# Moving the layer-norm centring of an attention stage from ScalarE to VectorE, and a copy to a later place in VectorE's order

## What is computed

```python
mod = (_silu(L0_c) @ L0_wmod).reshape(L0_c.shape[0], 6, 1, -1)
sa, ca, ga, sb, cb, gb = (mod[:, 0], mod[:, 1], ...)
h = _layernorm(x, axis=-1) * (1 + ca) + sa
x = x + ga * _L0_attn_ref(h, L0_attn_w_qkv, L0_attn_w_out)
h = _layernorm(x, axis=-1) * (1 + cb) + sb
x = x + gb * _L0_ffn_ref(h, ...)
```

## Time and profile before

| | |
|---|---|
| median of 3 runs | 1188.49 us (1187.46 to 1189.24) |
| the profiled execution's own time | 1188.49 us |
| span of its instructions | 1186.6 us |
| mean granted TensorE clock | 0.939 of full speed |
| busy share PE, DVE, ACT, POOL over the span | 90%, 79%, 78%, 74% |

### The profile page before, as it was taken

The page is one execution under the profiler, slowest core; times in us unless marked ns, Lnnn a source line. Parts: engine busy times, 40 slices in busy tenths (PEclk is TensorE's granted clock), DMA queues, the critical chain, the costliest instruction groups (busy, mean ns, idle before and its releaser), DMA issues. The chain is left out here.

```text
span 1186.6 us, 51662 instructions
## 1 busy us (share of the span) xinstructions
PE 1067.6 (90%) x18513; PEld 866.7 (73%) x18513; DVE 940.0 (79%) x4130; ACT 923.6 (78%) x3404; POOL 876.9 (74%) x732
## 2 busy tenths in 40 slices
PE   4799999999999999999999999748989985499994
PEld 2577877777777777877877877536867774488883
DVE  6888989889889888988989886547878764288885
ACT  2699999999999999999999997746866652266662
POOL 2788888888878888888888875454677677167777
PEclk9899999999999999999999998969988875699997
DMA  6777777776776777776767776262242122666210
GB/s 194 200 187 169 191 176 170 183 188 165 192 178 168 183 180 171 189 180 165 195 172 173 175 181 161 68 217 72 66 133 95 57 83 108 192 193 185 80 33 31
DMA packets 111036, 181.02 MB, mean 153 GB/s; under 512 B 19726, under 2 KB 64177, under 8 KB 110656
## 3 DMA queue, kind: packets, MB, share of 16 engines
q1 hardware_dynamic: 102944, 158.53, 52.4%
q0 software_dynamic: 6400, 16.82, 3.9%
q10 hardware_dynamic: 1440, 2.36, 0.7%
HBM read 35.20 MB, written 24.73 MB: 51 GB/s over the span
## 5 line engine op out<-in xcount | busy, mean ns | idle before, releaser
L621 POOL TENSOR_TENSOR qk<-mm,sw 128x1024 f32<-128x1024 f32 x128 | 305.9, 2390 | 92.5 <-DMA sw<-mm 92.1
L692 ACT ACTIVATE pr<-sm,mn 128x96 f32<-128x96 f32 x1024 | 368.5, 370 | 0.3 <-DVE mn L522 0.3
L503 DVE TENSOR_TENSOR mm<-bank,cos 128x512 f32<-128x512 f32 x256 | 175.1, 684 | 77.3 <-PE bank L325 64.8
L627 POOL TENSOR_TENSOR pr<-pr,ri 128x768 f32<-128x768 f32 x128 | 188.3, 1471 | 32.0 <-DVE ri L531 31.2
L692 ACT ACTIVATION_READ_ACCUMULATOR pr<-sm,mn 128x1 f32 x1024 | 201.6, 197 | 0.0
L522 DVE CUSTOM_DVE_ANT_0 sm<-bank,msk 128x96 f32<-128x96 f32 x1024 | 191.1, 252 | 1.6 <-PE bank L337 1.6
L504 DVE TENSOR_TENSOR mm<-bank,sin 128x512 f32<-128x512 f32 x256 | 174.1, 680 | 0.0
L702 ACT ACTIVATE pT<-bank 96x512 f32<-96x512 f32 x256 | 137.1, 586 | 15.3 <-PE bank L352 13.4
L368 PE MATMUL bank<-pT,vw 96*64 96x64 f32 x4096 | 148.3, 226 | 0.6 <-issue 0.6
L368 PEld LDWEIGHTS bank<-pT,vw 96*64 96x64 f32 x4096 | 130.6, 138 | 10.6 <-ACT oth L711 1.0
L337 PEld LDWEIGHTS bank<-qk 64*64 64x64 f32 x4096 | 90.8, 133 | 54.3 <-issue 53.1
(11 more groups left out here) (210 smaller groups left out, 2484.6 us busy)
## 6 DMA issues: line engine op xcount, KB each, us to landing
sw<-mm SPq DMA_DIRECT2D x512, 128.0 KB, 2.4
vw<-vn SPq DMA_DIRECT2D x128, 192.0 KB, 2.6
vw<-vn SPq DMA_DIRECT2D x128, 128.0 KB, 2.4
rr<-sorted_scratch SPq DMA_DIRECT2D x72, 192.5 KB, 2.8
vw<-vn SPq DMA_DIRECT2D x96, 64.0 KB, 2.4
xt<-in_x SPq DMA_DIRECT2D x16, 256.0 KB, 3.7
x_scratch<-x SPq DMA_DIRECT2D x16, 256.0 KB, 2.7
rr<-x_scratch SPq DMA_DIRECT2D x16, 256.0 KB, 3.0
```

The source lines that it names most:

```text
L503: dve.tensor_tensor(mm[s % 2][:, 0, j, :], PJ[u % 2][:, :], cos[:, :], ALU.mult)
L621: pool.tensor_tensor(qk[i % 2][:, :, 32:], mm[i % 2][:, 0, :, :], sw[i % 2][:, :, :], ALU.add)\
L627: pool.tensor_tensor(t, t, ri[i % 2][:, :].unsqueeze(2).to_broadcast([P, 8, WK]), ALU.mult)\
L692: ins = act.activation(pr[i % 2][:, h, p, :], ms_[i % 2][:, h, p, :], ACT.Exp, scale=-1.0, bias=mn[i % 2][:, h, p:p + 1], accum_out=sums[i ...
```

## The change

It has three parts in the steady loop, and one of small instructions.

1. `centre` for batches 1 to 15 leaves ACT, where it was four activations of 128x128 with scale `lnr` and bias `lnb`, two at the end of slot r = 0 and two at the end of r = 1. It becomes four DVE instructions of 128x128 (subtract the mean, multiply by `lnr`), all at the end of slot r = 1. Both the input `xt` and the output `hh` are read and written through a view that takes the 64 even channels first and then the 64 odd ones. Batch 0's centring was on DVE already and takes the new view too.
2. POOL no longer computes `lnb`: two small instructions for each batch go, and the counts of `s_ln` follow.
3. On DVE the copy of ACC to `yt` moves from ahead of the maxes to behind the reciprocal, in the same slot r = 6.

```diff
-        lnb = sbt(p1, "lnb", [P, 4])
                 def centre(b):
-                    dve.wait_ge(s_ln, 4 * b + 2)
+                    dve.wait_ge(s_ln, 2 * b + 2)
+                    if b:
+                        dve.wait_ge(s_xn, b)
                     for j in range(4):
-                        ins = dve.tensor_scalar(hh[:, j, :], xt[b % 4][:, j, :], mv[:, j, 0:1], lnr[:, j:j + 1],
-                                                ALU.subtract, ALU.mult)
+                        o, x = (v.rearrange("p (a k) -> p k a", k=2) for v in (hh[:, j, :], xt[b % 4][:, j, :]))
+                        ins = dve.tensor_scalar(o, x, mv[:, j, 0:1], lnr[:, j:j + 1], ALU.subtract, ALU.mult)
                     ins.then_inc(s_hc, 1)
...
-                    i = s - LO - 1
-                    if 0 <= i < NI and i % G == G - 1:
-                        b = i // G
-                        dve.wait_ge(s_op, i + 1)
-                        if b:
-                            dve.wait_ge(s_pj, pj_use[("yt", b - 1)] + 1)
-                        dve.tensor_copy(yt[:, :], ACC[:, :]).then_inc(s_yt, 1)
...
                         dve.reciprocal(ri[i % 2][:, :], sums[i % 2][:, :]).then_inc(s_ri, 1)
+                    i = s - LO - 1
+                    if 0 <= i < NI and i % G == G - 1:
+                        b = i // G
+                        dve.wait_ge(s_op, i + 1)
+                        if b:
+                            dve.wait_ge(s_pj, pj_use[("yt", b - 1)] + 1)
+                        dve.tensor_copy(yt[:, :], ACC[:, :]).then_inc(s_yt, 1)
                     if s % G == 6 and s // G + 1 < NB:
                         x_low(s // G + 1)
...
-                    if s % G == 3 and s // G + 2 < NB:
-                        layer_stats(s // G + 2)
+                    b, r = s // G + 1, s % G
+                    if b < NB:
+                        if r == 1:
+                            centre(b)
+                    if r == 3 and b + 1 < NB:
+                        layer_stats(b + 1)
...
                     pool.tensor_scalar(lnr[:, :], mv[:, :, 1], EPS, None, ALU.add).then_inc(s_ln, 1)
-                    pool.wait_ge(s_ln, 4 * b + 1)
+                    pool.wait_ge(s_ln, 2 * b + 1)
                     pool.tensor_tensor(lnr[:, :], lnr[:, :], nhalf[:, :], ALU.pow).then_inc(s_ln, 1)
-                    pool.tensor_scalar(lnb[:, :], mv[:, :, 0], -1.0, None, ALU.mult).then_inc(s_ln, 1)
-                    pool.wait_ge(s_ln, 4 * b + 3)
-                    pool.tensor_tensor(lnb[:, :], lnb[:, :], lnr[:, :], ALU.mult).then_inc(s_ln, 1)
                     yield
...
-                def centre(b, k):
-                    act.wait_ge(s_ln, 4 * b + 4)
-                    act.wait_ge(s_xn, b)
-                    for j in (2 * k, 2 * k + 1):
-                        ins = act.activation(hh[:, j, :], xt[b % 4][:, j, :], ACT.Identity, scale=lnr[:, j:j + 1],
-                                             bias=lnb[:, j:j + 1])
-                    if k:
-                        ins.then_inc(s_hc, 1)
-
...
-                    if b < NB and r in (0, 1):
-                        centre(b, r)
                     if b < NB and r in (3, 4):
                         squares(b, r - 3)
```

## The result

The changed kernel takes 1195.68 us (median of 19 runs, 1189.73 to 1203.61), the kernel before 1188.07 us in the same comparison (19 runs, 1184.42 to 1195.0). The ratio is 1.006, with a 95% interval from 1.0044 to 1.0077: slower, by 7.6 us between the medians. The prediction was 1193.0, in a range from 1187.0 to 1198.5, with slower as the likeliest sign. The profiled execution after has a span of 1197.4 us and took 1199.29 us, so it lies 3.6 us above the median, and its differences are a little larger than the typical ones.

The account below looks back on a forecast made before the run. The prediction took PE to bound the attention stage, at 5.46 us a slot. From 1188.49 us it added 2.9 (copy), 2.1 and 0.8 (burst held up by POOL), less 1.3 (lnb): 1193.0, range 1187.0 to 1198.5.

Parts of the forecast that it names:

- slower as the likeliest sign: Whole kernel: slower by more than about 0.2% had chance 0.56, against 0.32 for same and 0.12 for faster.
- PE sets the pace, the freed ACT time is worth nothing: Attention stage: PE runs without idle, 5.46 us a slot, and never waits directly for ACT; freed time gives nothing.
- The copy: Slot r = 6: L393 waits for the late copy; 2.1 us over 14 batches, 0.8 in the last, together 2.9.
- Exclusion: DVE can't run its burst beside POOL: Slot r = 1: the DVE burst waits while POOL's L627 runs; case total 1193.0, chance 0.45.
- The sign that the prediction took for it: DVE's TENSOR_SCALAR of 128 elements: 215 ns from SBUF, 272 from PSUM, read as a second path in use.
- a wait of 0.94: End of slot r = 1: the burst, ready at 573.91, waits 0.94 us for L627, which ends at 574.85.
- a late add and a longer r = 3 by 2.1 us: POOL's add before L352 of r = 4 may pass its 583.2 limit: PE stalls 0.15 us a batch, 2.1 over 14.
- The start-up, 0.8 us: First slots: a 1.1 us burst straight before the first add delays PE 0.8 us once, between 0 and 1.1.
- lnb, -1.3 us: POOL in r = 7: removing two instructions, 0.44 us a batch, shortens L352 waits; gain 1.3 us, at best 4.8.
- The view: DVE burst: taking every second element costs nothing extra, 344 ns an instruction; slow-view rival 1198.6, chance 0.10.
- The estimate from the Trainium skill: DVE burst: up to 2.5 ns for a lone element gives 0.1 us more an instruction, 0.4 a burst.
- Sum: Whole kernel: 1188.49 + 2.9 (yt) + 2.1 + 0.8 (burst held up by POOL) - 1.3 (lnb) = 1193.0.

Follow-up runs that it names:

- the early burst: Changed kernel with the copy in its old place and the burst between maxes and reciprocal of r = 1; ratio 1.0031.

## Why the prediction was right, and where its terms were off

- **PE sets the pace, the freed ACT time is worth nothing.** Right as far as the runs show. PE has no wait for ACT between 70 and 750 us in the trace of either kernel, and with ACT freed and no burst put in its place the ratio left at most 0.5 us of gain. The two lengths of the stage in the profile, 722.2 and 722.4 us, agree better than they need to: unchanged, it was also 725.5 and 726.7.
- **The copy.** Mechanism and place as forecast. Predicted 2.1 in r = 6 and 0.8 at the end; the profiles show 2.2 to 2.3 and 0.9; the timed pairs 4.1 with an error of 0.9. The copy itself was shorter than its row of before, 640 against 680 ns by the medians, and L392 followed it after 0.14 us in place of 0.06.
- **Exclusion: DVE can't run its burst beside POOL.** Right and shown: four instructions take 1.12 us when POOL is idle and 1.93 when L629 runs. The sign that the prediction took for it, 57 ns less out of SBUF than out of PSUM at 128 elements, could also have come from the two memories alone. Rows of the kernel before support it better: TENSOR_SCALAR out of SBUF takes 193 ns for 96 elements and 258 for 192, 0.68 ns an element, and COPY out of PSUM 269 for 128 and 680 for 512, 1.07 ns an element. Predicted was a wait of 0.94, measured 0.81. Predicted was a late add and a longer r = 3 by 2.1 us; in the profiles it is 2.7 and 1.6 with both parts, 1.1 and 0.9 with the centring alone, and 0.2 without the burst. After the change it falls on batches 1 to 4. One of them after the change, on PE:

```profile
131.88 0.50 PE L298 MATMUL bank<-wh,xh 128*128 128x512 f32 x1
136.54 0.65 PE L351 MATMUL bank<-ident,pr 64*96 64x64 f32 x16 [0.45 <-POOL pr L629]
138.20 0.50 PE L298 MATMUL bank<-wh,xh 128*128 128x512 f32 x1
```

  The distance is 6.32 in place of 5.46 us, and what ends it is L351's wait for POOL, as the prediction had it for that slot. Why only batches 1 to 4? The prediction's delay is in all 14: the swap transfers of r = 2 mostly start 0.85 us later, behind the held-up burst. But the delay alone was covered. POOL's add of that item, first in batch 2 and then in batch 6:

```profile
132.64 2.41 POOL L623 TENSOR_TENSOR qk<-mm,sw 128x1024 f32<-128x1024 f32 x1 [1.45 <-DMA sw<-mm]
```

```profile
314.37 2.41 POOL L623 TENSOR_TENSOR qk<-mm,sw 128x1024 f32<-128x1024 f32 x1
```

  In batches 1 to 4 after the change the last of the four transfers landed 2.57 to 3.41 us after its issue ended, and the add waited for it. In batches 5 to 14 it landed after 1.69 to 2.14, and the add came straight behind POOL's own work in nine of the ten. Before the change the landing took 1.71 to 2.26 in all 14. In the other profiles with the burst behind `otl`, too, r = 3 grew only in batches in which that landing took 2.3 us or more. So r = 3 grew where the later transfers also landed slowly, and why they did so in these four batches is open. The prediction had only the delay, spread over all batches as 0.15 us each; that its 2.1 us lies between the measured 1.6 and 2.7 is in part luck.
- **The start-up, 0.8 us.** Wrong. The first burst did meet the first add, and one instruction took 2412 to 2548 ns, but the first eight slots take 45.6 to 46.2 us in the kernels with the burst and 45.9 to 46.4 in the three profiles of the kernel before. It is worth nothing that these profiles can show; in the kernel before, too, DVE's next rope waited 2.54 us for that same add.
- **lnb, -1.3 us.** This is the term that failed. POOL's head start of 0.34 us reached the residual add and ended at SP: in all of the 13 batches the store waited for SP's own queue, and it left no earlier than before. The run without the burst left room for 0.5 us of gain at most. The prediction had part of the shift lost at the transfers; as far as the traces show, it was all of it.
- **The view.** Costs nothing, as taken. The estimate from the Trainium skill ("Vector Engine (DVE) Microarchitecture Reference", 5.2), 0.1 us more an instruction, is not borne out by the 339 ns.
- **Sum.** Forecast +4.5 us, measured 7.6 by the medians of the whole kernel and 7.8 by the means of the stage. By the positions the copy gave 3.1, r = 3 1.6 to 2.7, the start-up and lnb nothing, and slots 120 to 127, beyond the copy's 0.9, another 1.8 and 2.2. Without r = 2, that is 7.6 us in the whole kernel's profile and 6.9 in the stage's. So lnb accounts for 1.3 of the miss, the start-up for 0.8 the other way, and about 2 us are a term that the prediction did not have. That total fell inside its range because the range was wide. Two sizes stay open. Slots 120 to 127, where the constants of the second stage are loaded, took 46.84 and 47.69 us in the two profiles with both parts, 44.2 to 44.6 before, and 43.9 to 45.1 in the five with one part at its place in the changed kernel, but also 46.37 with the early burst and no late copy, so the growth does not need both parts. And r = 7 is 0.3 us longer over 14 batches in all kernels with the centring on DVE, even with one column of it. Why was not tested.

## What to carry to other kernels

Before moving work to an engine with idle time, look at what the neighbour that shares its memory path does at that very place: the same four instructions cost 1.12 or 1.93 us, by their place in the order alone. They were slow where both engines had just been released by the same reciprocal. Before moving a copy back, look for the first instruction that overwrites its source; here it ran 1.17 us after the copy, and a delay of 1.5 us was too long. And a head start for one engine is worth what the next queue lets through.

## What was unexpected of the hardware

One TENSOR_SCALAR of DVE on 128x128 elements, 339 ns by itself, took up to 2412 ns after the change and up to 2548 ns with the centring alone, when POOL's first add of 2.4 us ran: DVE stood still until that instruction was done, and ended 0.09 us after it. The rule of the Trainium skill ("SBUF — State Buffer", Who interferes with whom) for a DVE instruction that uses the port pair shared with GpSimd, that whoever comes second blocks for the whole instruction, agrees with the bursts behind L629, which POOL had begun 0.39 us earlier; the trace of before could not show it for an instruction with one SBUF input. At the first add the order is less clear: in the run of 2548 ns DVE's instruction is recorded as starting 0.08 us ahead of POOL's, and it was DVE that stood still. And an unchanged attention stage scattered by 3.5 us in r = 2 alone (79.14, 82.62, 82.62 us over 14 batches), by when the swap transfers of r = 1 landed; with the store and the load moved away, the same 14 distances agreed within 0.01 us.
